# DLRM tower on one core: GpSimd waits for a landing behind every eighth gather in place of every fourth

## What is computed

```
e = stack([tbl_f[ids[:, f]] for f in range(40)], axis=1)          # 2048 x 40 x 32
z[b, p] = e[b, i_p] @ B_p @ e[b, j_p]                             # 780 pairs i < j
h = concat([z, dense_ctx], axis=1)                                # 2048 x 796
h = relu(h @ W_top1 + b_top1)                                     # 512
h = relu(h @ W_top2 + b_top2)                                     # 256
y = h @ W_top3                                                    # 2048 x 1
```

## Time and profile before

| | us |
|---|---|
| median of 3 runs | 825.41 |
| profiled execution, its time | 827.26 |
| profiled execution, its span | 825.4 |
| TensorE busy | 753.9 (91%) |
| DVE busy | 584.1 (71%) |
| GpSimd busy | 410.7 (50%) |
| ScalarE busy | 190.9 (23%) |
| mean granted TensorE clock | 0.965 of 2.4 GHz |

### The profile page before, as it was taken

How to read it: one execution, slowest core, us unless ns; L and a number is a source line. 1 busy time by engine, 2 the same in 40 slices (tenths; PEclk the granted TensorE clock), 3 DMA queues, 4 the chain that set the end, 5 groups by cost and what they waited for, 6 DMA issues and landing times.

```text
span 825.4 us, 13618 instructions
## 1 busy us (share of the span) xinstructions
PE 753.9 (91%) x5648; PEld 240.5 (29%) x5648; DVE 584.1 (71%) x624; ACT 190.9 (23%) x301; POOL 410.7 (50%) x423
## 2 busy tenths in 40 slices
PE   4676968788899978999999999999999999999998
PEld 2222322222223222232333232232333223222233
DVE  7754857578885864787896787887895687777710
ACT  6414120212114113003122323102304122121002
POOL 4555455565565566665666465656665566600000
PEclk9878979799999999999999999999999999999999
DMA  4442644200002001002011101010111000000000
GB/s 111 101 68 37 87 57 92 50 11 12 10 10 35 12 11 30 10 12 35 11 29 14 34 10 29 11 36 11 21 20 14 12 10 11 12 3 1 0 1 0
DMA packets 61216, 22.32 MB, mean 27 GB/s; under 512 B 45048, under 2 KB 60341, under 8 KB 61155
## 3 DMA queue, kind: packets, MB, share of 16 engines
q1 hardware_dynamic: 47815, 14.57, 8.2%
q0 software_dynamic: 13312, 6.84, 6.8%
q10 hardware_dynamic: 28, 0.06, 0.0%
HBM read 21.36 MB, written 0.07 MB: 26 GB/s over the span
## 4 chain that ended last, share of the span: by engine, by line
PE 63%; POOL 14%; issue 10%; DMA 9%; DVE 2%; another core or an unknown queue 1%; ACT 1%; POOLq 0%; DVEq 0%
PE U L892 20%; PE bank_z L917 18%; POOL rows L547 14%; PE misc L943 13%; DMA rows<-in_tbl,idx 8%; PE misc L843 6%; PE U L943 3%; PE U L901 2%; PE U L866 2%; DVE prod L785 1%; DVE ones L749 0%; ACT x_T L592 0%; DMA idx<-in_ids 0%; PE bank_z L925 0%
## 5 line engine op out<-in xcount | busy, mean ns | idle before, releaser
L547 POOL DMA_INDIRECT rows<-in_tbl,idx x416 | 409.9, 985 | 311.2 <-DMA rows<-in_tbl,idx 199.6
L785 DVE TENSOR_TENSOR prod<-U,x_T 128x1024 f32<-128x1024 f32 x288 | 338.1, 1218 | 87.7 <-PE U L892 75.9
L917 PE MATMUL bank_z<-prod,select 128*32 128x512 f32 x1600 | 218.7, 619 | 2.4 <-issue 1.6
L892 PE MATMUL U<-x_T,W 32*128 32x512 f32 x1152 | 189.9, 667 | 10.5 <-ACT x_T L592 7.3
L843 PE MATMUL misc<-ones,tabs 125*32 125x512 bf16 x1680 | 126.6, 395 | 5.4 <-DVE ones L749 3.7
L749 DVE TENSOR_SCALAR ones<-idx_wide,row_of 125x2048 bf16<-125x2048 f16 (+1 forms) x160 | 108.3, 698 | 28.7 <-PE misc L843 15.7
L785 DVE TENSOR_TENSOR prod<-U,x_look 128x1024 f32<-128x1024 f32 x72 | 84.8, 1218 | 47.1 <-PE U L892 32.3
L943 PE MATMUL misc<-z,W 128*128 128x512 f32 x182 | 96.8, 633 | 0.0
L892 PEld LDWEIGHTS U<-x_T,W 32*128 32x128 f32 x1152 | 55.4, 190 | 107.9 <-issue 53.0
L843 PEld LDWEIGHTS misc<-ones,tabs 125*32 125x32 bf16 x1680 | 57.1, 100 | 96.1 <-issue 62.4
L917 PEld LDWEIGHTS bank_z<-prod,select 128*32 128x32 f32 x1600 | 31.9, 109 | 161.4 <-issue 110.8
(11 more groups left out here) (67 smaller groups left out, 274.5 us busy)
## 6 DMA issues: line engine op xcount, KB each, us to landing
rows<-in_tbl,idx POOLq DMA_INDIRECT x416
idx_wide<-idx_rows SPq DMA_DIRECT2D x7, 500.0 KB
idx_wide<-idx_rows SPq DMA_DIRECT2D x8, 375.0 KB
prod<-in_tbl SPq DMA_DIRECT2D x4, 156.2 KB
W<-in_W_top SPq DMA_DIRECT2D x35, 2.0 KB
W<-_L_rec_bilinear_matrices SPq DMA_DIRECT2D x4, 128.0 KB
W<-in_W_top SPq DMA_DIRECT2D x1, 512.0 KB
W<-_L_rec_bilinear_matrices SPq DMA_DIRECT2D x30, 4.0 KB
```

The source lines that it names most:

```text
L547: nc.gpsimd.indirect_dma_start(out=rows[:, n % R_SLOTS, t, f, :], out_offset=None, in_=tables[field][:, :], in_offset=bass.IndirectOffsetO ...
L785: last = nc.vector.tensor_tensor(to[:, :, m * N:(m + n) * N].rearrange("p r (m n) -> p r m n", m=n), U[:, at:at + 2, m * N:(m + n) * N].re ...
L892: last = nc.tensor.matmul(U[:, at + r % 2, m * N:(m + 1) * N], W[row, at_W:at_W + P], x_of(o, a)[row, :], start=True, stop=True, skip_grou ...
L917: last = nc.tensor.matmul(bank_z[r * DIM:(r + 1) * DIM, 0:N], sel, prod[:, (2 * g + r // 2) % P_SLOTS, r % 2, m * N:(m + 1) * N], start=(k ...
```

## The change

One constant is changed, and with it the condition in line 553: GpSimd goes on to the next gather without a wait seven times and waits behind the eighth. All other waits, the order of the gathers and all other engines' programs are as before.

```diff
--- before.py
+++ after.py
@@ -272,7 +272,7 @@
 assert all(at + 6 <= g or at == 0 for (o, c, f), at in DUE.items() for g in TURN_AT if (o, c) in TURN_AT[g])
 
 
-BURST = 4
+BURST = 8
 
 
 U_SLOTS = 3
```

## The result

Against the forecast of 793 us, the first comparison gave 879.0 us for the changed kernel (876.7 to 881.2, 4 runs) and 827.2 us for the one before (4 runs in all): a ratio of 1.066, interval 1.060 to 1.071, slower. The same two programs, compared again later, took 768.5 us (4 runs) against 820.0 us (7 runs), 0.940 (0.934 to 0.947), faster; two single runs on two more chips gave 767.2 and 769.1 us. Which chip the first comparison ran on isn't recorded. The forecast of a gain is wrong for the first comparison and too small for the others. Both need explaining; the first comparison first.

The account below looks back on a forecast made before the run. GpSimd standing still behind every fourth gather was taken to stall TensorE's transposes. Gains of 19.1 + 2.2 + 8.5 + 2.5 = 32.3 us off 825.4 gave 793 us, range 781 to 812.

Parts of the forecast that it names:

- What the change does to the gathers: GpSimd's gathers: nine removed landing waits bring them 19.1 us earlier by gather 72, bounds 12.0 to 26.3.
- rival A: First 150 us: long landing waits only move beside SP's loads; quiet ones pay 4.4 us by gather 72; 810 us, chance 0.12.
- B: GpSimd's issue: more than four gathers in flight lengthen gather records, so nothing is gained; 825 us, chance 0.05.
- C: GpSimd's issue: the second four of each eight take longer records, costing more than saved; slower, 862 us, chance 0.04.
- What TensorE gets of it: TensorE's transposes: stalls for gathers shrink, 19.1 us by gather 72, 2.2 at turn 7, 8.5 in the second block.
- what is late next: Once gathers are ahead, only TensorE's own work, paced by DVE's multiplies; GpSimd's other waits cost nothing.
- a stall of another kind: First-block sign of a wrong forecast: weights' landing or DVE's multiplies replace TensorE's gather stalls; no size given.
- TensorE's share: TensorE's total gain from earlier gathers and the faster clock: 32.3 us, low 22.7, high 41.5.
- the ceiling: High case for TensorE's gain: gathers up to 30.5 us earlier by gather 100, plus 8.5 and 2.5; 41.5 us, so 784.
- the one that was set to zero: Stretch from 322 us on: no transpose waits for a gather, TensorE's busy time covers the change; no gain counted.
- The clock: Second block: two 3 us slow stretches behind TensorE's stalls vanish, worth 2.5 us; nothing taken for the first block.
- The Trainium skill's fixed cost: GpSimd's gather DMAs: about 2.04 us each, making a removed wait worth 1.74 us and the total 3.4 us less.

Follow-up runs that it names:

- e5: The changed kernel (wait behind every eighth gather) run again unchanged on another chip: 768.5 us, ratio 0.940 to the kernel before.
- e6: The kernel before (wait behind every fourth gather) run again unchanged for its trace: 820.7 us, one run.
- e1: Against the kernel before, GpSimd waits behind every sixteenth gather instead of every fourth: 759.1 us, ratio 0.924.
- e4: Against the kernel before, waits behind every eighth gather, with seven chained tiny memsets as a pause in the middle of each eight: 803.4 us, ratio 0.979.
- e11: Waits behind every eighth gather with seven chained tiny memsets mid-eight, against the kernel before, repeated on another chip: 801.6 us, one run.

## Why the prediction was right or wrong

**What the change does to the gathers: right.** 19.1 us were forecast by gather 72. Gather 73 started 20.9 us earlier in the first comparison and 24.9 us earlier in e5 against e6:

```profile
125.39 0.94 POOL L547 DMA_INDIRECT rows<-in_tbl,idx  x1 [5.17 <-DMA rows<-in_tbl,idx]
```
```profile
150.28 0.94 POOL L547 DMA_INDIRECT rows<-in_tbl,idx  x1 [3.61 <-DMA rows<-in_tbl,idx]
```

Both lie within the 12.0 to 26.3 of the bounds; the middle between them was a choice and not worked out. Part of the long waits did move, as rival A has it, but a small part: the nine waits that were kept up to there sum to 30.3 us in place of 25.4 in the first comparison and to 29.4 in place of 25.3 in e5 against e6, so 4 to 5 us moved and over 20 came back, where A let 4.4 come back. Records of gathers did not grow (980 to 988 ns in the four traces), so neither B nor C in the form that I gave it happened, although the first comparison ended on C's side, at 879 us.

**What TensorE gets of it, and what is late next: these steps failed in the first comparison.** The prediction gave TensorE 19.1 us by the turn of gather 72, since it "can't be earlier than its gather" and would otherwise follow it; then, once the gathers are ahead, only "TensorE's own work" was to be late. At that turn TensorE was 23.1 us later and not 19.1 earlier. The first traces show something else in its place: the hand-over from TensorE to DVE and ScalarE. Its increments arrive up to 12.4 us late while GpSimd issues gathers, the copies of transposed chunks start late, and TensorE stands for ScalarE (30.8 us at line 892, 27.9 of them before the turn of gather 100; 7.3 in the kernel before) with its clock down (0.938). To this come the hiccups inside looks. The prediction had named "a stall of another kind" in the first block as what would make it wrong, but had thought of weights and DVE's multiplies, and gave slower 0.04 for another reason. From the turn of gather 176 on, where the prediction had nothing gained and nothing lost, the two first traces do take the same 431 us; but e5 takes 411 (281.86 to 693.02), so in the first comparison that stretch was held up too, before and after the change alike.

The same program without late increments takes 765.5 us of span against 874.6, 109 us less. The late increments, the hiccups and the missing records are what I found to differ between the two; that the late increments turn the gain into a loss is read from the rows, where TensorE, ScalarE and DVE stand for them, and no run turned them on or off. For the kernel before the two traces differ by 6.5 us of span (825.4 and 818.9), which fits late increments hidden under the gathers' own lateness: there TensorE mostly had to wait for gathers anyway. The trace of before could so look healthy, and it misled me twice. I read "remote" waits of 45, 24 and 9 us on a one-core kernel as labels that mean nothing, and I read the missing gather stalls after 322 us as slack of the gathers, when e6 has them.

**Why only there.** Shown: the same two programs have 131 and 173 late increments in the first traces and none in the later traces, on four chips; so it is neither the change nor the program alone. That the first traces' late increments come of GpSimd's gathers is argued, not shown: they end by the last gather; of those over 0.3 us late, 141 of 211 (before) and 137 of 244 (changed) arrive in GpSimd's pauses, over 0.5 us behind a gather's record and ahead of the next one, which make up 23% of the time that it gathers. It fits T1, that a run without a pause holds them and that eight hold them longer than four, but e1, e4 and e11, meant to test it, ran without the effect. A rival stands untested: that the recording was disturbed and held the engines, since the two traces with late increments are those that lack 38% (before) and 47% (changed) of the semaphore records; every run here was recorded, with its granted clock, so none shows the time without that. Whether the effect belongs to one chip, to the moment, to the recording, or to something that the traces don't show, stays open: it came back on none of the four chips, so no variant could be tried under it.

**TensorE's share: too small in the runs without late increments.** There the gain is 53.4 us of span (818.9 to 765.5) where 32.3 was forecast and 41.5 was the ceiling. By its own terms: by gather 72, 19.1 were forecast and 24.9 measured (the transposes at 150.16 and 125.26 us). Up to the turn of gather 176, 32.3 were forecast and 37.7 measured (319.56 and 281.86 us). The remaining 15.7 us lie behind that, where I had put nothing: in e6 TensorE still waits for gathers at 500.60 and 676.94 us, 8.2 us together, and its clock is at 1.2 GHz for 17 us from 319 us on, worth nearly half of that; in e5 neither happens. Together that is near the 15.7. So the mis-sized terms are the one that was set to zero, by 15.7 us, and the gathers' 19.1, by 5.8. The reason for the first is argued above: in the trace that I read, TensorE was late enough for the gathers.

**The clock** was counted only in the second block. In e5 its mean is 0.987 against 0.950 in e6, and over the first 150 us 0.93 against 0.85: it goes with the stalls, in the first block as well.

**The Trainium skill's fixed cost** of a DMA (page "DMA: Bandwidth & Descriptors", section "Anatomy of one DMA — SWDGE (gpsimd) path", about 2.0 us and its bytes) would have put the sum 3.4 us lower. The prediction laid it behind the gather's record. Counted from the start of the record, a gather in e6 lands after 2.4 us (median behind 170 us) against the page's 2.04, and a quiet wait is still 1.6 to 1.9 us. What the Trainium skill's same page says in "Queues, rings and completion order" and "Issuing engines are not separate DMA queues" on sharing the engines spoke for rival A; e5 and e6 show 4 to 5 us of such moving, and down to no wait at all the kernel only gets faster.

## What to carry to other kernels

When a releaser in the waits can't exist ("remote" on one core), find out what it is before predicting: here it stood for an engine's own increments arriving late, and it hid behind the very wait that the change removes. A count of the records that a trace holds, against another trace of the same program, is worth its minute: here nearly half of those of semaphores were missing. A stall that is absent from a trace proves slack only if the waiting engine was not itself held up. And a loss of 7% in four agreeing runs was a gain of 6% in the next comparison: agreement between the runs of one comparison doesn't carry over to another, so a surprise is first repeated unchanged, with its trace, before any theory is tested on variants.

## What the runs showed of the hardware that I had not expected

- In the first comparison TensorE's semaphore increments arrive up to 12.4 us behind the end of the matmul that makes them, while those of DVE and ScalarE in the same trace are on time (0 late of 436 and 121 recorded), and DVE and ScalarE start just behind the late ones. In such stretches TensorE also stands still for 0.34, 1.02 or 1.03 us inside a look. The cause is open.
- The traces with late increments also lack records of semaphores: 776 of TensorE's against 849 for the same program elsewhere, 436 of DVE's against 585, 121 of ScalarE's against 148, 3,162 of the gathers' landings against 6,652. Whatever holds the increments may hold the records too; I can't tell which comes first.
- Waiting for a landing behind gathers is of no use here at any spacing, in the runs without late increments: from two gathers to none, each thinning of the waits made the kernel faster, 977 to 753 us, and the mean record of a gather stayed between 974 and 990 ns.
